# First projection of an attention kernel: query parts stored once, values for two to four chunks, two generations of parts, and down products that wait tile by tile

## The reference, cut to what matters

```
qkv = q @ in_proj_weight.T + in_proj_bias          # 4096 x 768
qh = qh / sqrt(d)                                  # 16 heads, d = 16
scores = einsum('bhid,bhjd->bhij', qh, kh)         # 4096 x 4096 per head
bias = take_along_axis(qh @ rel_pe.T, clip(j - i, -64, 64) + 64)
attn = softmax(scores + bias);  out = attn @ vh;  out @ out_w.T + out_b
```

```
h = layernorm(shift_token(x)) @ w1 + b1            # 256 -> 2 * 682
a, g = split(h);  x = x + (a * gelu(g)) @ w2 + b2  # 682 -> 256
```

## Time and profile before

| | us |
|---|---|
| median of 3 runs | 5642.28 (5639.37 to 5642.45) |
| profiled execution, its own time | 5645.27 |
| span of the profiled execution | 5643.6 |
| project_heads, from the start to POOL's first instruction of the next block | 234.2 |
| DVE reductions of the large attention (L745), busy | 2684.3 |
| PE busy, share of the span | 92% |

### The profile page before, as it was taken

The page is one execution under the profiler, slowest core; times in us unless marked ns, Lnnn a source line. Parts: engine busy times, 40 slices in busy tenths (PEclk is TensorE's granted clock), DMA queues, the critical chain, the costliest instruction groups (busy, mean ns, idle before and its releaser), DMA issues. The chain is left out here.

```text
span 5643.6 us, 113158 instructions
## 1 busy us (share of the span) xinstructions
PE 5194.8 (92%) x34272; PEld 2739.5 (49%) x34272; DVE 4145.7 (73%) x8689; ACT 3115.0 (55%) x4539; POOL 959.2 (17%) x711
## 2 busy tenths in 40 slices
PE   6399999999999999999999999998599989899988
PEld 3233333333333333333333333334488867788866
DVE  4288888888888888888888888871477744677755
ACT  3256666666666666666666666661266621455521
POOL 0111111111111111111111111100233310233211
PEclk7589999999999999999999999995699999999989
DMA  6612121111111221111221211111200000000000
GB/s 166 143 40 56 48 56 53 48 54 53 49 53 48 55 57 47 54 53 49 53 56 50 55 47 49 49 43 32 94 1 0 0 16 0 17 0 0 0 38 23
DMA packets 205156, 254.48 MB, mean 45 GB/s; under 512 B 72270, under 2 KB 134036, under 8 KB 203284
## 3 DMA queue, kind: packets, MB, share of 16 engines
q1 hardware_dynamic: 201220, 232.98, 14.9%
q0 software_dynamic: 3856, 20.45, 1.4%
HBM read 210.73 MB, written 42.47 MB: 45 GB/s over the span
## 5 line engine op out<-in xcount | busy, mean ns | idle before, releaser
L745 DVE TENSOR_REDUCE group_max<-shared_ps 128x1 f32<-128x512 f32 x4096 | 2684.3, 688 | 575.4 <-PE shared_ps L469 472.8
L622 ACT ACTIVATE probs<-scores 128x1024 f32<-128x1024 f32 x2048 | 2012.3, 1021 | 1042.0 <-PE scores L495 662.9
L469 PE MATMUL shared_ps<-keys,max_queries 96*128 96x512 bf16 x4096 | 1434.6, 385 | 2.0 <-issue 1.7
L495 PE MATMUL scores<-queries,keys 98*128 98x512 bf16 (+3 forms) x4096 | 1214.9, 371 | 86.6 <-ACT probs L622 85.6
L510 PE MATMUL out_ps<-probs,values 128*17 128x512 f32 x8192 | 1083.1, 601 | 0.4 <-ACT probs L622 0.4
L469 PEld LDWEIGHTS shared_ps<-keys,max_queries 96*128 96x128 bf16 x4096 | 395.6, 97 | 1116.4 <-DVE group_max L745 507.8
L215 POOL TENSOR_TENSOR near_window<-near_bias,one_f 128x1536 bf16<-128x1536 f32 x128 | 351.5, 2747 | 2942.1 <-DVE max_parts L739 2297.4
L495 PEld LDWEIGHTS scores<-queries,keys 98*128 98x128 bf16 x4096 | 359.4, 98 | 462.8 <-ACT probs L622 236.9
L521 PE MATMUL shared_ps<-block_q,block_table 96*128 96x32 bf16 x4096 | 271.5, 233 | 65.9 <-POOL block_q L406 65.9
L521 PEld LDWEIGHTS shared_ps<-block_q,block_table 96*128 96x128 bf16 x4096 | 231.3, 114 | 172.5 <-issue 123.2
L1168 POOL TENSOR_TENSOR norm<-norm,layer_expo 128x16 f32<-128x16 f32 x64 | 186.2, 2910 | 706.4 <-DVE norm L1555 706.4
(11 more groups left out here) (194 smaller groups left out, 5828.2 us busy)
## 6 DMA issues: line engine op xcount, KB each, us to landing
keys<-k_parts SPq DMA_DIRECT2D x384, 96.0 KB, 2.1
values<-v_wide SPq DMA_DIRECT2D x128, 272.0 KB, 2.8
keys<-k_parts SPq DMA_DIRECT2D x384, 64.0 KB, 2.0
keys<-k_parts SPq DMA_DIRECT2D x128, 132.0 KB, 2.4
q_stack<-part SPq DMA_DIRECT2D x96, 128.0 KB
k_parts<-part SPq DMA_DIRECT2D x96, 128.0 KB
queries<-q_stack SPq DMA_DIRECT2D x128, 96.0 KB, 2.2
max_queries<-q_stack SPq DMA_DIRECT2D x128, 96.0 KB, 2.3
```

Source lines behind the costliest of these rows:

```text
L469: mm = pe.matmul(bank, max_queries[par][:, t * P:(t + 1) * P], keys[par][0:ROWS, (t + TPC * g) * P:(t + TPC * (g + 1)) * P], start=True, s ...
L495: mm = pe.matmul(out[:, 0:cut], keys[par][:, c * P:(c + 1) * P], queries[par][:, 0:cut], start=True, stop=True)
L622: act.activation(probs[s % 4][:], scores[s % 2][:], ACT.Exp).then_inc(exp_done, 1)
L745: dve.tensor_reduce(group_max[par][:, k:k + 1], bank, AX.X, ALU.max).then_inc(max_read, 1)
```

## The change

**In project_heads.** The q parts are stored once: `q_parts` takes the three parts of a q variant with three DMAs, as `k_parts` does. The part buffer has two generations, chosen by the parity of the chunk, and ACT waits once a chunk, for all stores of the chunk two before. `v_stage` holds all 32 tiles, so that nothing waits for its stores, and the values go out after chunk 3 (for chunks 0 to 3), after chunk 5 and after chunk 7 (two chunks each), with runs of 1088, 544 and 544 bytes. POOL loads each input chunk on its own wait. The loops are written out, without registers. ACT makes the exact numbers of a variant ahead of the high part of the variant before it.

**In attend.** `queries`, `max_queries` and `head_q` are now put together from `q_parts` by six DMAs of 16 rows each, where one DMA of 96 rows did it.

**In local_layers.** `go_down` waits for each tile of `hidden` ahead of its matmul, for w = 0.

```
-        part = sb("part", [P, 3, 6, CH], BF16)
-        v_stage = sb("v_stage", [P, HEADS, TPC, VW])
+        part = sb("part", [P, 2, 3, 6, CH], BF16)
+        v_stage = sb("v_stage", [P, HEADS, TILES, VW])
...
+        V_SPANS = {3: (0, 4), 5: (4, 6), 7: (6, 8)}
...
-                    pool.wait_ge(values_done, m * 2 + 1)
+            for n in range(CHUNKS):
+                if n >= 2:
+                    pool.wait_ge(values_done, n - 1)
...
-                    if unit < 2:
-                        for t, which in enumerate(Q_PARTS):
-                            sp.dma_start(q_stack[heads, t * D:(t + 1) * D, bass.ds(col, CH)],
-                                         part[:, which, v, :]).then_inc(parts_stored[v], 16)
...
+                    parts = q_parts if unit < 2 else k_parts
+                    for which in range(3):
+                        sp.dma_start(parts[heads, which * D:(which + 1) * D, side:side + CH],
+                                     part[:, par, which, v, :]).then_inc(parts_stored[par], 16)
+                if n in V_SPANS:
+                    sp.wait_ge(v_staged, n + 1)
+                    first, last = V_SPANS[n]
...
+                if n >= 2 and v == 0:
+                    act.wait_ge(parts_stored[n % 2], STORES * (n // 2))
...
             def load_queries(n, par):
                 h, c = place(n)
-                sp.dma_start(queries[par][0:ROWS, :], q_stack[bass.ds(h, 1), :, bass.ds(c * CH, CH)]
-                             ).then_inc(queries_in[par], 16)
+                for t, which in enumerate(Q_PARTS):
+                    sp.dma_start(queries[par][t * D:(t + 1) * D, :],
+                                 q_parts[bass.ds(h, 1), which * D:(which + 1) * D, bass.ds(c * CH, CH)]
+                                 ).then_inc(queries_in[par], 16)
...
-                pe.wait_ge(S.hidden_ready, g * HT + HT + 1)
...
-                        if w == 0 and i == HT - 1:
-                            pe.wait_ge(S.hidden_ready, g * HT + HT + 2)
+                        if w == 0:
+                            pe.wait_ge(S.hidden_ready, g * HT + i + 3)
```

More of the change, by code:

```diff
@@ L41 @@
 K_RUNS = (3, 2, 1)
+QUERY_DMAS = 16 * len(Q_PARTS)
 TERMS = len(Q_PARTS)
@@ L53, with project_heads @@
 UG = BLOCK_U // 2
-def project_heads(nc, x_T, w_in_T, b_in, pe_edges, q_stack, k_parts, v_wide):
+def project_heads(nc, x_T, w_in_T, b_in, pe_edges, q_parts, k_parts, v_wide):
     with ExitStack() as ctx:
@@ L114, in _ @@
             sp.dma_start(v_bias[:], b_in[2 * E:3 * E].rearrange("(a n) -> a n", a=1)).then_inc(consts_in, 16)
-            with sp.Fori(0, CHUNKS) as n:
-                col = n * CH
+            for n in range(CHUNKS):
+                par = n % 2
                 for v, (unit, _) in enumerate(VARIANTS):
@@ L119, in _ @@
                     heads = slice(GROUP * (unit % 2), GROUP * (unit % 2 + 1))
-                    if unit < 2:
-                        for t, which in enumerate(Q_PARTS):
-                            sp.dma_start(q_stack[heads, t * D:(t + 1) * D, bass.ds(col, CH)],
-                                         part[:, which, v, :]).then_inc(parts_stored[v], 16)
[L124 to L136, removed]
+                    side = n * CH if v in (0, 1, 2, 4) else n * CH + N
+                    parts = q_parts if unit < 2 else k_parts
[5 more added lines that the diff above has]
+                    first, last = V_SPANS[n]
+                    for again in range(2):
+                        sp.dma_start(v_wide.rearrange("h p (t e) -> p h t e", e=VW)
+                                     [:, :, first * TPC + again * TILES:last * TPC + again * TILES, :],
+                                     v_stage[:, :, first * TPC:last * TPC, :]).then_inc(v_stored, 16)
+            for par in range(2):
+                sp.wait_ge(parts_stored[par], STORES * (CHUNKS // 2))
+            sp.wait_ge(v_stored, 32 * len(V_SPANS))
         @block.tensor
@@ L163, in _, with make_exact @@
             act.preload_act_table(ACT.Identity)
[L164 to L167, removed]
             act.wait_ge(bias_made, 1)
             act.wait_ge(ones_set, 2)
[L170 to L182, removed]
+            def make_exact(n, v):
+                unit, b = VARIANTS[v]
+                act.wait_ge(units_done, n * 4 + unit + 1)
+                if n > 0:
+                    act.wait_ge(rest_done, (n - 1) * 6 + v + 1)
+                act.activation(exact[:, v, :], unit_ps[unit][:], ACT.Identity,
+                               bias=bias[:, b:b + 1], scale=D ** -0.5 if unit < 2 else 1.0
+                               ).then_inc(exact_done, 1)
@@ new lines, in make_high @@
+            def make_high(n, v):
+                if n >= 2 and v == 0:
+                    act.wait_ge(parts_stored[n % 2], STORES * (n // 2))
+                act.wait_ge(exact_done, n * 6 + v + 1)
+                act.activation(part[:, n % 2, 0, v, :], exact[:, v, :], ACT.Identity).then_inc(hi_done, 1)
+            for n in range(CHUNKS):
+                for v in range(6):
+                    make_exact(n, v)
+                    if v > 0:
+                        make_high(n, v - 1)
+                make_high(n, 5)
+                act.wait_ge(values_done, n + 1)
@@ L183, in _ @@
                 for half in range(2):
-                    ins = act.activation(v_stage[:, :, 2 * half:2 * half + 2, 0:D],
+                    ins = act.activation(v_stage[:, :, n * TPC + 2 * half:n * TPC + 2 * half + 2, 0:D],
                                          value_ps[half][:].rearrange("p t (h d) -> p h t d", d=D),
```

105 lines of the change are left out of this document (57 added, 48 removed).

## The result

| | before | after |
|---|---|---|
| median of these runs, us | 5642.36 (4 runs) | 5563.41 (4 runs, 5558.54 to 5567.6) |
| profiled execution, its own time | 5645.27 | 5562.97 |
| span | 5643.6 | 5561.3 |
| POOL's first instruction of attend | 234.2 | 162.3 |
| from there to the first maximum of attend | 48.9 | 60.1 |

The ratio is 0.9856 (95% interval 0.9839 to 0.9873). The forecast was 5559.0 us, 4.4 less, so its likeliest case came true. The stages of the two traces give -71.9, +11.2, +3.1 and -23.0 us, together -80.6 of the -82.3 by which the spans differ; the rest lies between join_heads' input rows and the first up product. The forecast had -77.4, +10.3, 0 and -16.2. That its sum, -83.3, came within 1.0 us of the spans is in part luck: project_heads, the start of attend and the loop together gave 9.5 us less than forecast, the other stretches 8.5 us more.

The account below looks back on a forecast made before the run. It took project_heads to be bound by the DMA engines. Terms: -77.4 (project_heads) + 9.2 + 1.1 (start of attend) - 16.2 (feed-forward) = -83.3 us, from median 5642.3 to 5559.0 us; range 5545 to 5592.

Parts of the forecast that it names:

- likeliest case: Whole kernel: the forecast itself, 5559.0 us, with 5549 to 5571 as its own range; chance 0.60.
- The bound of project_heads: project_heads before the change: bound by the DMA engines, 25.5 us of a 27.0 us chunk; the rest idle time.
- step 1: project_heads, first store: moves from 15.94 to 17.9 us, by a longer v_stage memset and ACT's changed order.
- step 3: project_heads, value stores: three pairs with longer runs take 28.9 us, where 60.8 are spent now.
- the line: Value stores: straight line through 29.7 ns (272-byte run) and 42.9 (1024), giving 34.5 for 544 and 44.0 for 1088.
- rival (a): Value stores in project_heads: runs priced by their bytes, 23.3 us in place of 28.9, so 5553.4; chance 0.12.
- Rival (b): Value stores in project_heads: cost by each 272 bytes, no gain, 60.8 us, so 5590.9; chance 0.08.
- rival (c): project_heads: TensorE at half clock becomes the bound, stage ends near 216, time 5618 us; chance 0.05.
- rival f: Change fails, for instance PE starves on inputs in project_heads, saving half the stage or less: 5598 or more; chance 0.04.
- the issue term: Start of attend: 20 more loads on SP ahead of table_rows, 0.46 us an issue, cost 9.2 us.
- rival (e): Loop of attend: loads come late; with 2.1 us exposed in each of 126 turns, 265 us more, 5824; chance 0.03.
- Feed-forward: local_layers: PE's 17.2 us wait for hidden goes, less 1.0 for more waits: 16.2 us less; bounds 0 to 17.2.

Follow-up runs that it names:

- the 128-row stores: Changed kernel with q_parts laid out part by part in DRAM, so a q store has 128 rows as slowest dimension, not 8 heads: 5556.61 us, ratio 0.9838.
- the doubled stores: Changed kernel with each q part stored a second time, to a tensor that nobody reads: 5596.32 us, ratio 0.9907.
- the shorter start: Changed kernel with 128-row q stores and earlier table_rows and head_q, plus table_rows before keys, head 1 after the first block, table cut before memsets: 5541.66 us.

## Why the prediction was right, and where its sizes were off

**The bound of project_heads** was read rightly, from the first value stores on; before them PE sets the pace of the changed kernel. The part stores run on eight engines at 0.686 us each; the 128-row stores and the doubled stores move the stage end by 9.7 and 33.2 us, as this says. The rest were idle times of the input pairs and of one generation of parts: both come back (11.9 and up to 28.2 us) when their edit is undone.

**First store** (step 1): forecast 17.9, measured 19.1. The term mis-sized is the memset. It was scaled from 0.96 us to 7.7, and took 7.31, but began at 2.90, not at 1.31 as its short predecessor, so PE began at 10.31.

**Values** (step 3): forecast 28.9. What is left of the stage when every other term stands as forecast and the first store and the last landing as measured (161.5, 0.8 ahead of POOL's first instruction) is 161.5 - 1.5 - 19.1 - 98.8 - 8.4 - 1.3 = 32.4 us, so 3.5 more. From the second pair to the third, 115.62 to 148.18, it took 32.56 us; less 36 stores of parts, 24.7, a pair with runs of 544 bytes costs 7.9 where the line gave 8.8. Twice that leaves 16.6 for the first pair, with runs of 1088 bytes; from the first pair to the second (42.24 us, less 24.7 and two input loads, 2.8) it is 14.7. So 15 to 17, where the line gave 11.3: the term that was mis-sized most.

The price of the first pair is not all a price of its runs: the six slow microseconds from 90 us lie in it, at a mean of 146 GB/s, which against 191 is a loss of 1.4 us. Why they were slow is open.

By whole pairs, 272-byte runs (1.11 MB in 6.15 us) moved 181 GB/s and both longer ones 260 to 300: between 272 and 544 bytes the time for a byte falls by a third, and above that it is level. In stretches where only values move it is not level: 1088-byte runs went at 365 GB/s (88 to 90 us, above), 544-byte runs at 296:

```profile
156.00:158.00 2.00, 0.00 (x0) 0.00 (x0) 0.00 (x0) 0.00 (x0) 0.00 (x0) 0.50 1.18 296
```

So rival (a) is half right. Short runs are dear by the byte, as it had it and as the Trainium skill says of transfers under 512 bytes ("DMA: Bandwidth & Descriptors", "Specifications"); whether there is a step at 512 or a fixed cost in every run, three lengths do not tell. Its price, the 382 GB/s of twice eight engines, was not to be had: in steps of 2 us from 76 to 90 the rate was 312 to 383, with the highest beside an input load. The pairs took 32.4 us, where (a) had 23.3 and the straight line 28.9. Rival (b), 60.8 us, is refuted.

The forecast had called 7.6 us a pair spent before. Between stores of parts it adds 6.1 to 6.2, so pooling gives 19.9 and not 31.9. This did not move the forecast of the stage, since that was built up from its own terms and not as a difference.

**The rest of the stage.** The 5.5 us by which it ended late are these 3.5, 1.2 of the first store, and 0.8 between the last landing and POOL's first instruction, which the sum did not have. The 32.4, and so the 3.5, are what is left over and hold every error of the other terms. PE ran without a gap from 12 to 112 us at a granted clock of 1.00, so rival (c) did not occur, and no wait of PE for input was left (rival f).

**Start of attend**: the issue term was exact, 9.2 forecast and 9.1 measured. POOL's loads cost 2.1, not 1.1, within the bounds of 0.6 to 3 (its twelve loads took 5.78 us and the block waited 2.22 for them). **The loop**: nothing lost. The +3.1 us lies within the spread of all the kernels (3526.6 to 3546.6), of which a kernel with the loop unchanged has the largest; so rival (e) is refuted and SP's idle time was real cover. Its waits in the loop fell from 2410.9 us in all to this line and 0.2 us:

```profile
SPq L342 <- PE scores L517: 1783.0, 377, 6.1
```

That is 5.0 us less a turn, so ten loads took 5.0 and five 2.5, where the forecast had 2.1 (and 2.3 by its own 0.46 an issue). With it, the 265 us of rival (e) would have been 315.

**Feed-forward**: forecast -16.2, measured -19.9 in the two layers' feed-forward (246.0 to 234.0, and 243.2 to 235.3). The mechanism was right; the size was read from the wait view, which lists 1.57 us for a gap that by start-to-start was 2.20 - 0.46 = 1.74. The same holds over all 16 batches: the time from the last up product's start to the first down product's falls from 23.6 us in all to 3.7, by 19.9, where the wait view lists 17.2. The 1.0 us allowed for more waits was not there: the 24 matmuls take 5.99 us, before 6.03.

Another -3.1 us lie between the two feed-forwards, where the edit does nothing. There TensorE's clock differs: over the same 60 us ahead of the second layer's first up product the mean granted clock is 0.74 before and 0.86 after. With this edit the stretch takes 564 to 565 us in every trace, without it 567.3 and 571.1. Whether the edit has a part in that is open, and the forecast had no such term.

## What to carry to other kernels

Look at the DMA share of a stage that stores: a plateau near one half can mean, as here, that the shape of the transfer on the DRAM side leaves the other engines idle, and a longer slowest dimension may give them back without moving a byte less. Where one DMA is split into several, count the issues ahead of the first dependent step on that queue, not only the time of the loads; the loop may take them for nothing while a start pays for every one. Build a stage up from its own terms and from prices with the same neighbours in the queue: what a store costs at the end of a stage is not what it adds between others. And take a wait that is to vanish from start to start, not from the wait view.

## What was not expected of the hardware

- Sixteen DMA engines together moved 312 to 383 GB/s in the 1088-byte value stores (steps of 2 us from 76 to 90, a mean of 351 at share 1.06 with an input load among them), some 22 each, where eight moved 191, 24 each. As that pair ran out the rate fell to 115 to 183 GB/s for six microseconds while SP was issuing stores; why is open.
- A pair of 272-byte-run stores does not move evenly. Between stores of parts it adds 6.1 us, 24 ns a run, where a run of 1024 bytes costs 42.9. Alone it went at 147 GB/s at a share above 1 in one kernel and at 198 over two microseconds of another (139 to 141 us, values each by themselves).
- Six small loads (`table_rows`) took 11.9 us to be usable while the loads of keys, values and both heads of `head_q` were in flight, and 5.0 when they came last. With only queries and one head ahead of them, in the shorter start, the last of them landed 6.7 us after the first issue (162.72 to 169.41). So most of it comes with the keys, the values and the second head; which of them costs it was not tested apart.
- A store over 128 rows takes SP 0.51 us to issue, one of 8 x 16 rows 0.64; the six behind the first value pair take 15.35 us together.
